# Transposes by pairs in a recurrent stage, and a mixture's last second products moved into the next stage

## The reference, cut to what matters

```
x = x + 0.5 * L0_ffn(layernorm(x))   # mixture of 8 experts, 2 per token, hidden 176, shared hidden 352
x = x + L0_attn(layernorm(x))        # gated recurrence over 256 steps
x = x + 0.5 * L0_ffn(layernorm(x))
x = x + 0.5 * L1_ffn(layernorm(x))   # mixture of 16 experts, 2 per token, hidden 128, shared hidden 128
x = x + L1_attn(layernorm(x))        # attention inside each sequence
x = x + 0.5 * L1_ffn(layernorm(x))
```

## Time and profile before

| | us |
|---|---|
| median of 3 timed runs | 882.19 |
| lowest and highest | 880.62 and 882.26 |
| the profiled execution's own time | 884.11 |
| its span in the profile | 882.3 |
| PE, DVE, ACT, POOL busy, share of the span | 88%, 57%, 48%, 34% |
| the chain of waits, share by engine | PE 69%, DVE 15%, ACT 5%, DMA 3%, issue 3%, POOL 2% |
| mean granted clock | 0.954 |

### The profile page before, as it was taken

The page is one execution under the profiler, slowest core; times in us unless marked ns, Lnnn a source line. Parts: engine busy times, 40 slices in busy tenths (PEclk is TensorE's granted clock), DMA queues, the critical chain, the costliest instruction groups (busy, mean ns, idle before and its releaser), DMA issues.

```text
span 882.3 us, 14560 instructions
## 1 busy us (share of the span) xinstructions
PE 779.4 (88%) x3982; PEld 553.5 (63%) x3982; DVE 500.8 (57%) x1737; ACT 421.7 (48%) x1028; POOL 299.6 (34%) x316
## 2 busy tenths in 40 slices
PE   5989999998888989999983899998899885999991
PEld 2446777754456446777752578887677663578881
DVE  4566322368757665322369663236897867662247
ACT  3822334316553822343336336552688777245540
POOL 0571433400000471433305717551011133627550
PEclk9999999999999999999995799998999999899996
DMA  8843333199999523333186345536000011245528
GB/s 297 251 149 109 114 108 96 54 295 371 344 344 342 181 107 114 103 108 102 55 290 270 107 121 180 156 108 209 1 1 2 1 49 46 86 143 177 158 98 287
DMA packets 102367, 135.28 MB, mean 153 GB/s; under 512 B 11367, under 2 KB 90727, under 8 KB 101735
## 3 DMA queue, kind: packets, MB, share of 16 engines
q1 hardware_dynamic: 87894, 95.05, 33.9%
q0 software_dynamic: 14400, 39.34, 12.6%
HBM read 56.23 MB, written 78.12 MB: 152 GB/s over the span
## 4 chain that ended last, share of the span: by engine, by line
PE 69%; DVE 15%; ACT 5%; DMA 3%; issue 3%; POOL 2%; SPq 1%; DVEq 0%; POOLq 0%; ACTq 0%
PE bank L1021 19%; PE bank L1042 12%; PE bank L915 10%; PE bank L1091 5%; PE bank L1001 4%; PE bank L1032 3%; PE bank L928 3%; PE bank L1141 2%; POOL slot_rows L507 2%; DVE X L1318 2%; DVE st L1336 2%; DMA Y<-f_result_rows 1%; PE bank L1221 1%; DVE X L1322 1%; PE bank L855 1%
## 5 line engine op out<-in xcount | busy, mean ns | idle before, releaser
L507 POOL DMA_INDIRECT f_result_rows<-arena x172 | 164.8, 958 | 224.6 <-ACT arena L665 124.4
L507 POOL DMA_INDIRECT slot_rows<-XN,slots x128 | 123.9, 968 | 244.8 <-DMA slot_rows<-zeros 118.7
L1021 PE MATMUL bank<-w,arena 128*128 x688 | 202.6, 417 | 0.9 <-ACT arena L652 0.9
L1648 DVE COPY arena<-bank 88x128 f32<-88x128 f32 (+1 forms) x250 | 65.0, 285 | 213.8 <-PE bank L1032 213.6
L1021 PEld LDWEIGHTS bank<-w,arena 128*128 128x128 f32 x688 | 129.4, 190 | 31.4 <-issue 1.6
L1042 PE MATMUL bank<-w,arena 88*128 (+1 forms) x500 | 136.5, 381 | 0.0
L915 PE MATMUL bank<-XT,f_s 128*128 128x512 f32 (+1 forms) x256 | 118.1, 609 | 2.7 <-DMA f_s<-in_f_s 1.1
L659 ACT ACTIVATE arena<-bank 128x128 f32<-128x128 f32 (+1 forms) x172 | 50.8, 295 | 116.6 <-PE bank L1021 116.6
L665 ACT ACTIVATE arena<-bank 128x256 f32<-128x256 f32 x172 | 65.9, 383 | 73.1 <-PE bank L1042 72.3
L1042 PEld LDWEIGHTS bank<-w,arena 88*128 88x128 f32 (+1 forms) x500 | 81.4, 190 | 5.6 <-issue 0.8
L915 PEld LDWEIGHTS bank<-XT,f_s 128*128 128x128 f32 (+1 forms) x256 | 46.2, 188 | 57.7 <-issue 53.5
(11 more groups left out here) (168 smaller groups left out, 1121.6 us busy)
## 6 DMA issues: line engine op xcount, KB each, us to landing
slot_rows<-zeros SPq DMA_DIRECT2D x16, 2176.0 KB, 17.9
arena<-slot_rows SPq DMA_DIRECT2D x172, 128.0 KB, 2.1
XN<-f_result_rows SPq DMA_DIRECT2D x32, 256.0 KB, 5.3
Y<-f_result_rows SPq DMA_DIRECT2D x32, 256.0 KB, 6.1
w<-in_f_w SPq DMA_DIRECT2D x1, 4096.0 KB, 16.9
w<-in_f_w SPq DMA_DIRECT2D x1, 2816.0 KB
f_result_rows<-arena POOLq DMA_INDIRECT x172, 2.5
X<-in_x SPq DMA_DIRECT2D x4, 512.0 KB, 5.7
```

The lines of the kernel that those rows point to most:

```text
L507: pool.indirect_dma_start(out=dst, out_offset=bass.IndirectOffsetOnAxis(ap=idx, axis=0), in_=src, in_offset=None).then_inc(done.sem, 16)
L1021: last = pe.matmul(bank[2 + q % 2][:, 0:2 * m.H], xsT[q % 2][:, k, :], L["w13"][:, k, bass.ds(e, 1), :], start=(k == 0), stop=(k == KD - 1))
L1648: last = dve.tensor_copy(hT[q % 2][0:kp, k, :], bank[4 + q % 2][0:kp, k * P:(k + 1) * P])
```

## The change

Two things. In the recurrent stage the next group's four tiles are transposed in pairs: two tiles fill bank 0 and one copy of ACT takes both, as the mixture stages already do. The first pair stands behind the second half's f projection and the second behind its i projection; ACT copies the first pair ahead of the sigmoid of i and the second behind it. Second, the second wide mixture's second products of group 3 leave the end of that stage. 34 idle transposes stand there instead; the products stand in the narrow stage, on PE between `logits_back` and `positions` of group 1, and their additions move on DVE from `combine` of group 1 to `combine` of group 3.

The diff, cut to its core (`shared_down` becomes a function that takes the stage; its body stays as it was):

```
@@ -376,6 +376,10 @@
+        def passed_on(s, g):
+
+            return g == NG - 1 and s["kind"] == "f0" and s["next"]["kind"] == "f1"
@@ ACT, recurrence
                         act.activation(g_in[c], f, ACT.Sigmoid, scale=-1.0).then_inc(s["in_"].sem, 1)
+                        if c and g + 1 < NG:
+                            copy_pair(s, g + 1, 0, 0)
                         act.wait_ge(*s["i_psum"](n + 1))
                         act.activation(g_si[c], i, ACT.Sigmoid).then_inc(s["si"].sem, 1)
                         if c and g + 1 < NG:
-                            copy_xT(s, g + 1, 0, banks=1)
-                            copy_xT(s, g + 1, 1, banks=1)
+                            copy_pair(s, g + 1, 1, 0)
...
-                    if g + 1 < NG:
-                        copy_xT(s, g + 1, 2, banks=1)
-                        copy_xT(s, g + 1, 3, banks=1)
...
-                for t in range(GT):
-                    copy_xT(s, 0, t, banks=2)
+                copy_pairs(s, 0, (0, 1))
@@ PE, mixture
-                        if s["prev"] is not None and s["prev"]["mixes"]:
-                            pe.wait_ge(*s["prev"]["shared_added"](NTT))
...
                         logits_back(s, g)
+                    if nk == 1 and g == 1 and s["prev"]["mixes"]:
+                        shared_down(s["prev"], NG - 1)
...
                 else:
+                    if s["prev"]["mixes"]:
+                        pe.wait_ge(*s["prev"]["shared_added"](NTT))
                     shared_up(0)
...
                 for g in range(HELD[s["kind"]], NG):
-                    shared_down(g)
+                    if not passed_on(s, g):
+                        shared_down(s, g)
+                if passed_on(s, NG - 1):
+                    keep_busy(34, 0)
@@ PE, recurrence
-                    pe.wait_ge(*s["xT"](GT * (g + 1)))
+                    pe.wait_ge(*s["xT"](2 * (g + 1)))
...
-                            if g + 1 < NG and c and k:
-                                transpose_x(s, g + 1, 2 * k - 2, banks=1)
-                                transpose_x(s, g + 1, 2 * k - 1, banks=1)
+                            if g + 1 < NG and c and k < 2:
+                                pe.wait_ge(*s["xT"](2 * (g + 1) + k))
+                                transpose_pair(s, g + 1, k, 0)
...
-                transpose_group(0)
+                transpose_pair(s, 0, 0, 0)
+                transpose_pair(s, 0, 1, 1)
@@ DVE
-                if g == late:
+                if passed_on(s, g):
+                    shared_add(s, g)
+                elif g == late and not passed_on(s, NG - 1):
                     for held in range(HELD["f0"] if s["next"] and s["next"]["kind"] == "h" else NG - 1, NG):
                         shared_add(s, held)
```

More of the change, by code:

```diff
@@ L298, in stage @@
             nd = BY_DVE[kind]
-            copies = NTT if kind == "h" else 2 * NG
+            copies = 2 * NG
             totals = dict(stats=NTT, aggr=NG, stdev=NG, rstd=NG, xn_dve=NG * nd, xn_act=NG * (GT - nd),
@@ L592, in copy_pairs @@
                 copy_pair(s, g, 1, banks[1])
-            def copy_xT(s, g, t, banks=2):
-                act.wait_ge(*s["xT_psum"](GT * g + t + 1))
-                act.activation(XT[:, :, bass.ds((GT * g + t) * P, P)],
-                               bank[t % banks][:, 0:D].rearrange("p (k n) -> p k n", k=KD),
-                               ACT.Copy).then_inc(s["xT"].sem, 1)
             def logits(s, g):
@@ L832, in _ @@
             loaded(pe, "const")
-            def transpose_x(s, g, t, banks=2):
-                i = GT * g + t
-                normalised(pe, s, g, t)
-                if i >= banks:
-                    pe.wait_ge(*s["xT"](i - banks + 1))
-                for k in range(KD):
-                    last = pe.transpose(bank[t % banks][:, k * P:(k + 1) * P], XN[:, i, k * P:(k + 1) * P], ident[:, :])
-                last.then_inc(s["xT_psum"].sem, 1)
             def keep_busy(n, b):
@@ L901, in positions, with shared_down @@
                 last.then_inc(s["pos_psum"].sem, 1)
+            def shared_down(s, g):
+                L = LAYERS[s["kind"]]
+                m = L["m"]
+                nk = len(m.KS)
+                pe.wait_ge(*s["hid"](nk * (g + 1)))
+                for h in range(2):
+                    if g >= HELD[s["kind"]] + 2:
+                        pe.wait_ge(*s["shared_added"](GT * (g - 2) + 2 * (h + 1)))
+                    elif 0 < g < HELD[s["kind"]]:
+                        pe.wait_ge(*s["shared_added"](GT * (g - 1) + 2 * (h + 1)))
+                    for t in (2 * h, 2 * h + 1):
+                        for c, kp in enumerate(m.KS):
+                            last = pe.matmul(down_bank(s, g, h)[:, t % 2 * D:(t % 2 + 1) * D],
+                                             f_HT[0:kp, (g * nk + c) % HTS, t * P:(t + 1) * P],
+                                             L["s2"][0:kp, c, :], start=(c == 0), stop=(c == nk - 1))
+                        last.then_inc(s["down"].sem, 1)
             def mixture(s):
@@ L917, in shared_up @@
                     last.then_inc(s["up"].sem, 1)
-                def shared_down(g):
-                    pe.wait_ge(*s["hid"](nk * (g + 1)))
-                    for h in range(2):
-                        if g >= HELD[s["kind"]] + 2:
-                            pe.wait_ge(*s["shared_added"](GT * (g - 2) + 2 * (h + 1)))
-                        elif 0 < g < HELD[s["kind"]]:
-                            pe.wait_ge(*s["shared_added"](GT * (g - 1) + 2 * (h + 1)))
-                        for t in (2 * h, 2 * h + 1):
-                            for c, kp in enumerate(m.KS):
-                                last = pe.matmul(down_bank(s, g, h)[:, t % 2 * D:(t % 2 + 1) * D],
-                                                 f_HT[0:kp, (g * nk + c) % HTS, t * P:(t + 1) * P],
-                                                 L["s2"][0:kp, c, :], start=(c == 0), stop=(c == nk - 1))
-                            last.then_inc(s["down"].sem, 1)
                 def tile_lists():
```

7 lines of the change are left out of this document (2 added, 5 removed).

## The result

The changed kernel takes 887.7 us (median of four runs, 886.0 to 888.7), against 881.4 us (880.2 to 882.3) for four runs of the kernel before on the same chip: ratio 1.006, 95% interval 1.0041 to 1.0079, so 3.6 to 7.0 us slower. Forecast was 2.6 us slower.

A forecast was written before the change was run, and what follows sets the result against it. Hand-overs with ACT bound the recurrent stage, the zero fill and scatters the second wide stage, DVE's choices the narrow stage. Terms -1.0 + 3.6 = +2.6 us on 882.19 gave 884.8 us; own range 883.3 to 886.6, over cases 881.6 to 887.3.

The forecast's parts named there:

- Recurrent stage, 6.4 us earlier: Paired transposes remove PE's copy waits and two slow-clock stretches; group 3's first projection at 243.4 instead of 249.85; bounds 1.8 to 8.
- Rival (d): DVE and ACT hold the recurrent stage, gain there 1.8, PE keeps its clock; 884.3 us; chance 0.60 together with the forecast.
- Swallowed by the fill: Second wide stage: zero fill still lands at 296.1, so scatters end at 336.36 and rows are asked for at 337.99.
- Rival (b): The fill is not the last thing holding the second wide stage; 6.4 us survive, sum -2.8, 879.4 us; chance 0.08.
- Gain before the gapless tiles, 1.0: Second wide stage's first expert tiles: gain of 2.2 at full clock, reduced to 1.0 by slow clock; ends 0 and 2.2.
- the clock term: First expert tiles: PE at 1.2 GHz for 3.4 us after idling; half is 1.7, less 0.5 falling into waits.
- The sign given for it: Profile should show PE idle 4 to 5 us ahead of the first expert tile, with clock 0.50 behind it.
- rival (c): PE at 1.2 GHz through the whole pause (delay 5.6), cold into the experts (gain 0): +6.9, 889.1 us; chance 0.10.
- PE's delay in the pause, 2.3 (0.6 to 5.6): Narrow stage: 24 products take 6.7 to 7.2 us in a 4.54 us pause, making group 1's positions 2.3 us late.
- Rival (a): PE gets full clock in or before the pause, delay 0.6; sum about +0.3, 882.5 us; chance 0.17.
- Additions, 1.3: Narrow stage: DVE's four additions, 1.33 us, delay the choice of group 2, which had no idle time ahead.
- Rival (e): Transposes do not hold PE's clock, so the narrow stage's group 0 is late by 0.4; 885.2 us; chance 0.05.

The follow-up runs named there:

- part 1 alone: Only the paired transposes of the recurrent stage, against the kernel before: 881.3 against 882.4 us, ratio 0.9986; on another chip 915.9 against 913.0 us, ratio 0.9999.
- part 2 alone: Only the late second products, their additions and 34 idle transposes, old recurrence, against the kernel before: 884.9 against 882.4 us, ratio 1.0031; another chip 911.7 against 913.0.
- the run with PE kept busy ahead of the rows: Paired transposes only, plus 40 idle transposes between PE's last shared product and the second wide stage's first rows, against the kernel before: 914.8 against 913.5 us, ratio 1.0019.
- the run without idle transposes: Late second products and additions with the old recurrence, without the 34 idle transposes, against the kernel before: 915.9 against 913.5 us, ratio 0.9999.

## Why the prediction was right, and where it was short

On the chip of the first comparison direction, place and mechanisms came out as forecast; the time, 887.7 us, is 0.4 us past the upper end of the range, 887.3, and the ratio's 5.3 us are twice the 2.6 forecast.

- **Recurrent stage, 6.4 us earlier:** 6.2 in the first pair of profiles, 4.0 between the medians of seven and six profiles. The means are right: no copy wait over 1.03 us, no slow clock behind group 0. The number is in part luck: 1.8 of the 6.4 is a slow stretch that only the profile before has. Rival (d), a gain of 1.8, falls.
- **Swallowed by the fill:** right. First scatter at 296.4 net, row load at 338.2 net, before 296.11 and 337.99. Rival (b), in which the fill isn't binding, falls on this chip.
- **Gain before the gapless tiles, 1.0:** 0.2 us lost in the trace, -2.8 to +0.4 us in the timed runs of part 1 alone. The step that was mis-sized is the clock term. I took 1.7 less 0.5 us from the earlier trace rows, 3.4 us at half clock. Here it lasted from PE's first row to about 344.6, and the transposes and products of the first two tiles took 7.0 us (1.46, 2.71, 0.63, 2.19) instead of 3.7 at the later tiles' durations (0.60, 1.35, 0.38, 1.35): 3.3 us more. From the first row to the gapless part (345.32) it is 6.4 us, where the forecast had 4.3 at full clock and 1.2 for the slow one; the 2.2 had the DVE wait's end in it already. It stayed inside the stated ends, 0 and 2.2, all but 0.2. The sign given for it, 4 to 5 us of idle PE ahead of the first tile, was 2.98 us in the changed kernel and 5.00 in part 1 alone. Half of rival (c), cold into the experts with no gain, is thus what happened; its other half, a pause at half clock throughout, is not.
- **PE's delay in the pause, 2.3 (0.6 to 5.6):** 1.8 in the changed kernel, 2.4 in part 2 alone. Products of 6.73 and 7.31 us, forecast 6.7 to 7.2. (By its own terms, 6.7 to 7.2 less a pause of 4.54, the forecast's delay is 2.2 to 2.7 and not 1.9 to 2.5, and 5.8 and not 5.6 at half clock throughout.) Rival (a), a warm pause, falls, and keeping PE busy with idle transposes did not make one.
- **Additions, 1.3:** 1.16 in the changed kernel, 1.51 alone.
- **Rival (e)**, the page's rule in the Trainium skill, "TensorE: Matmul & The Clock Gate", Part 4: the clock was 1.00 through 40 idle transposes in the run with PE kept busy ahead of the rows, and rose under 26 of them in the earlier trace rows. The trace disagrees with the page for these fp32 transposes. Yet what hangs on it here is nothing: group 0's eight transposes run at half clock with or without the 34 ahead of them.
- **The sum:** in the first pair of profiles the changed kernel is +3.1 us, net, at the narrow stage's row load and +3.25 at the end; the timed runs of each part add up to +1.5 us (-1.2 and +2.7). The first timed comparison says 3.6 to 7.0. Where these meet, at 3 to 4 us, is the likeliest value, an estimate, but about 2 us of the first comparison's 5.3 are in no row that I can point to. It has four runs a side, within 2.1 and 2.7 us, and the profiled execution before, 884.11, already lies outside its side's. The part of the program behind the narrow stage's row load, which no edit touches, took 370.4, 370.6, 367.5, 368.0, 372.3 and 370.5 us in the six profiles of the ruler's table, and single runs of the kernel before spread from 877.6 to 885.7. This stays open. The chance of 0.65 for slower holds for a chip without the stops; for the other two chips the forecast had no case.

## What to carry to other kernels

Time gained ahead of a transfer that was started earlier still is no gain: follow it to the next thing that lands, and look in the same edit whether that can leave the path (here by waiting for the half of the fill that is used). What such an edit gives must be read where it is to run: here it is measured only on chips where it also made stops shorter. One profile is one draw: the stretch from which 6.4 us were forecast was 2 to 3.4 us longer in it than in six others with the same code. Work put into an engine's pause costs its duration at the clock that the pause has left it with, and queues whatever stands behind it on that engine; a pause of 4.5 us did not hold 5.2 us of work, which took 6.7. A shift of 0.3% needs more than one chip: the same two kernels compared at 1.006 on one and at 0.9975 on another.

## What the runs showed of the hardware

- Two of the chips ran the same program 31 us (3.5%) longer, and their profiles have stops of 2 to 11 us in which an engine has no instruction running and no releaser that the profile knows; that these make up the 31 us was not added up. The profile's instruction queues show 70 to 73 records in each profile, on the chips with stops and without. The Trainium skill, "Runtime: NRT & Kernel Launch", section "Instruction fetch mechanics", says that every engine fetches its program in blocks through a queue of its own, a cost "mostly hidden". That the stops are such fetches would fit, but no run here shows it.
- In the run without idle transposes PE fell idle at 464.6; its granted clock was still 1.00 over 466 to 469 and was 0.55 over 469 to 472, and PE's next work began at 471.66.
- At 338.89 and at 471.70 dense work that began at 1.2 GHz kept it for 5.7 us and for about 3 us: the first behind 2.98 us of idle time, the second behind transposes and logits with gaps under 1 us. The one row that I had sized the first from, 3.4 us, could not bound it.
